# Attention and feed-forward layer: score tiles in runs of three, two and three pairs, and the products with V of two steps together

## The reference, cut to what matters

```python
q, k, v = split(x @ w_qkv.T + b_qkv)          # 16 heads of 16 channels
q, k = rope(elu(q) + 1), rope(elu(k) + 1)
attn = softmax(einsum('bhnd,bhmd->bhnm', q, k) / 4) # 1024 x 1024 for each head
a = einsum('bhnm,bhmd->bhnd', attn, v) + depthwise_conv3(v)
x = layernorm(x + a)
h = relu(s0 * [x, -x] @ W0) * 2               # 512 -> 1024, weights +1 or -1
h = relu(s1 * h @ W1) * 2                     # 1024 -> 1024
x = layernorm(x + s2 * h @ W2)                # 1024 -> 256
```

## Time and profile before

| | us |
|---|---|
| median of 3 runs | 2095.07 (2094.85 to 2098.65) |
| the profiled execution | 2094.53 |
| its span, first to last instruction | 2092.4 |
| PE busy | 2043.8 (98%), clock granted 0.985 on the mean |
| DVE busy | 1685.7 (81%) |
| ACT busy | 1489.0 (71%) |
| POOL busy | 1013.3 (48%) |

### The profile page before, as it was taken

The page is one execution under the profiler, slowest core; times in us unless marked ns, Lnnn a source line. Parts: engine busy times, 40 slices in busy tenths (PEclk is TensorE's granted clock), DMA queues, the critical chain, the costliest instruction groups (busy, mean ns, idle before and its releaser), DMA issues.

```text
span 2092.4 us, 43715 instructions
## 1 busy us (share of the span) xinstructions
PE 2043.8 (98%) x17150; PEld 802.9 (38%) x17150; DVE 1685.7 (81%) x3094; ACT 1489.0 (71%) x2867; POOL 1013.3 (48%) x583
## 2 busy tenths in 40 slices
PE   5999999999999999999999999999999999999998
PEld 3132323343433434334343343434343343434355
DVE  8989988788887988888887888878888788888143
ACT  3399888766877678776787767777687766867642
POOL 2968287614757158462585328661475704300010
PEclk7699999999999999999999999999999999999999
DMA  5001210020010200021000200002001010000000
GB/s 199 20 17 47 72 24 31 22 72 13 15 37 31 80 16 16 30 77 42 9 27 27 89 22 17 29 16 99 12 17 37 29 62 17 17 9 29 1 21 21
DMA packets 40429, 76.87 MB, mean 37 GB/s; under 512 B 15024, under 2 KB 19488, under 8 KB 37280
## 3 DMA queue, kind: packets, MB, share of 16 engines
q1 hardware_dynamic: 34496, 49.97, 8.3%
q0 software_dynamic: 5184, 23.07, 3.0%
q10 hardware_dynamic: 544, 1.05, 0.1%
HBM read 46.27 MB, written 25.17 MB: 34 GB/s over the span
## 4 chain that ended last, share of the span: by engine, by line
PE 86%; DVE 8%; ACT 3%; issue 1%; SPq 0%; DMA 0%; POOL 0%; POOLq 0%; ACTq 0%
PE unit_banks L761 27%; PE unit_banks L625 22%; PE o_bank L670 22%; PE unit_banks L697 5%; PE unit_banks L774 5%; DVE maxima L1032 5%; ACT probs L855 2%; PE unit_banks L685 2%; PE unit_banks L635 2%; DVE hT L1101 1%; PE unit_banks L678 1%; ACT rows L943 0%; DMA lepe_rows<-in_b_v 0%; ACT work L897 0%; DVE rows L1161 0%
## 5 line engine op out<-in xcount | busy, mean ns | idle before, releaser
L1032 DVE TENSOR_REDUCE maxima<-unit_banks 128x1 f32<-128x512 f32 x2048 | 1302.5, 682 | 285.4 <-PE unit_banks L625 281.7
L855 ACT ACTIVATE probs<-unit_banks 128x512 f32<-128x512 f32 x2048 | 1115.5, 605 | 491.1 <-PE unit_banks L635 487.6
L625 PE MATMUL unit_banks<-k_stack,q_stack 48*128 48x512 f16 x2048 | 636.5, 388 | 6.2 <-DVE maxima L1032 2.7
L635 PE MATMUL unit_banks<-q_stack,k_stack 50*128 50x512 f16 x2048 | 634.0, 383 | 5.3 <-ACT probs L855 3.2
L670 PE MATMUL o_bank<-probs,v_pair 128*32 128x256 f32 x8192 | 565.3, 387 | 4.0 <-issue 4.0
L761 PE MATMUL unit_banks<-h0T,w 128*128 128x512 f16 x2048 | 480.2, 380 | 0.1
L1439 POOL TENSOR_TENSOR attn<-o_rows_sb,rden 128x256 f32<-128x256 f32 x63 | 39.2, 622 | 743.1 <-DVE rden L1045 739.5
L670 PEld LDWEIGHTS o_bank<-probs,v_pair 128*32 128x32 f32 x8192 | 207.0, 109 | 306.3 <-issue 206.0
L625 PEld LDWEIGHTS unit_banks<-k_stack,q_stack 48*128 48x128 f16 x2048 | 121.8, 94 | 433.2 <-issue 241.3
L761 PEld LDWEIGHTS unit_banks<-h0T,w 128*128 128x128 f16 x2048 | 188.6, 98 | 249.3 <-issue 55.6
L1104 DVE SCALAR_TENSOR_TENSOR h1T<-unit_banks,h1T 128x512 f16<-128x512 f32 x128 | 87.3, 682 | 77.9 <-ACT h1T L919 77.8
(11 more groups left out here) (151 smaller groups left out, 1677.8 us busy)
## 6 DMA issues: line engine op xcount, KB each, us to landing
rows<-in_x POOLq DMA_DIRECT2D x8, 1024.0 KB, 6.3
q_stack<-q_scratch SPq DMA_DIRECT2D x128, 64.0 KB, 2.0
k_stack<-k_scratch SPq DMA_DIRECT2D x128, 64.0 KB, 2.0
work<-in_xT SPq DMA_DIRECT2D x7, 1024.0 KB, 8.1
q_scratch<-parts POOLq DMA_DIRECT2D x14, 512.0 KB, 3.3
k_scratch<-parts POOLq DMA_DIRECT2D x14, 512.0 KB, 3.2
out<-rows SPq DMA_DIRECT2D x7, 1024.0 KB, 4.9
q_stack<-q_scratch SPq DMA_DIRECT2D x128, 32.0 KB, 1.9
```

Of the source, the lines that this page charges most:

```text
L625: nc.tensor.matmul(units.out(unit), q_stack[row:row + STACK, r, t * P:(t + 1) * P], k_stack[row:row + STACK, r, half * 512:(half + 1) * 51 ...
L635: nc.tensor.matmul(units.out(unit), k_stack[row:end, r, kt * P:(kt + 1) * P], q_stack[row:end, r, half * 512:(half + 1) * 512], start=True ...
L855: nc.scalar.activation(probs[:, 2 * (kt % 2) + h, half * 512:(half + 1) * 512], units.out(unit), ACT.Exp, scale=exp_regs[2 * (n % PAIRS) + ...
L1032: nc.vector.reduce_max(maxima[:, v // T % 2, h * T + t, half:half + 1], units.out(unit), AXIS_X)\
```

## The change

PE now goes through the steps two at a time. With s odd, and a "pair" one S and one T tile: dense work and own units of step s come behind the first pair of step s; those of step s + 1 come behind its third pair; the products with V of steps s - 1 and s come together behind the second pair of step s + 1. From dense piece to dense piece and to the products this gives runs of two and of three pairs: dense work of s, two pairs, dense work of s + 1, three pairs, products of two steps, three pairs, dense work of s + 2. The function `between(s, i)` names the step whose dense work stands ahead of pair i of step s. A step that has no dense work takes one half product in its place (`early_products`), and the rest follow behind the second pair (`products_behind`).

The readers' orders follow: ACT takes what ended in the dense work ahead of the exponential of the pair behind it, and DVE takes it behind the row maximum of that pair. Side work comes once a step. "max rows" is at kt = 6 instead of 5. `probs` has five halves instead of four, `v_pair` a ring of three pairs instead of four (`copy_v` is one pair less ahead), and `o_rows_sb` one buffer instead of two. The number of matmuls, exponentials, maxima and DMAs is the same, and there are still seven banks.

The diff, unchanged lines and hunks that only rename left out:

```diff
@@ -42,6 +42,8 @@
+V_RING = 3
+HALVES = 5
@@ -65,7 +67,7 @@
-O_ROWS_STEP, RECIPROCAL_STEP, MAX_ROWS_STEP = 2, 3, 5
+O_ROWS_STEP, RECIPROCAL_STEP, MAX_ROWS_STEP = 2, 3, 6
@@ -73,7 +75,7 @@
-COPY_V_AT = {3: (0, 1, 2, 3, 4, 7), 1: (7,), 5: (7,)}
+COPY_V_AT = {3: (0, 1, 2, 3, 4, 5), 1: (7,), 5: (7,)}
@@ -184,14 +186,31 @@
-def done_within(s):
-    return [u for u, part in DEALT[s][:-1] if ends_unit((u, part))] if 0 <= s < STEPS else []
-def done_behind(s):
-    return [u for u, part in DEALT[s][-1:] if ends_unit((u, part))] if 0 <= s < STEPS else []
+def done_in(s):
+    return [u for u, part in DEALT[s] if ends_unit((u, part))]
+def between(s, i):
+    return s if s % 2 == 1 and i == 1 else s + 1 if s % 2 == 1 and i == 3 and s + 1 < STEPS else None
+def early_products(s):
+    if DEALT[s] or s == 0:
+        return []
+    if s % 2 == 1:
+        return [2 * s - 2] if (s - 1) % T != 0 else []
+    return [2 * s - 4 + len(early_products(s - 1))]
+def products_behind(s):
+    return range(2 * s - 4 + len(early_products(s - 1)) + len(early_products(s)), 2 * s) if s > 0 else ()
@@ -223,29 +242,31 @@
-    for s in range(STEPS + 1):
-        for h in range(2):
-            for half in range(2):
-                if s + T + LEAD < STEPS:
-                    yield ("S", s + T + LEAD, h, half), True, True, True
-                if s < STEPS:
-                    yield ("T", s, 1 - h, half), True, True, True
-            if h == 0:
-                for u in done_behind(s - 1):
+    for s in range(STEPS):
+        for i in range(4):
+            w = between(s, i)
+            if w is not None:
+                for u in own_units(w):
+                    yield u, True, True, True
+                for u, part in DEALT[w]:
+                    yield u, part == 0, ends_unit((u, part)), False
+                for _ in early_products(w):
+                    yield PV, False, False, False
+            if s + T + LEAD < STEPS:
+                yield ("S", s + T + LEAD, i % 2, i // 2), True, True, True
+            yield ("T", s, 1 - i % 2, i // 2), True, True, True
+            if w is not None:
+                for u in done_in(w):
...
-                for u in own_units(s) if s < STEPS else ():
-                    yield u, True, True, True
-                for u, part in DEALT.get(s, ()):
-                    ends = ends_unit((u, part))
-                    yield u, part == 0, ends, ends and u not in done_behind(s)
-            elif s > 0:
-                yield PV, False, False, False
+            if i == 1 and s % 2 == 0:
+                for _ in products_behind(s):
+                    yield PV, False, False, False
...
-WRITING = {"S": 0.25, "T": 0.25, "PV": 0.9, "O rows": 0.15, "max rows": 0.15, "scale": 0.1, "bound": 0.1}
+WRITING = {"S": 0.25, "T": 0.25, "PV": 0.45, "O rows": 0.15, "max rows": 0.15, "scale": 0.1, "bound": 0.1}
@@ -344,12 +365,12 @@
-        v_pair = sb("v_pair", [P, RING, T, 2, 32], F32)
+        v_pair = sb("v_pair", [P, V_RING, T, 2, 32], F32)
...
-        probs = sb("probs", [P, 4, N], F32)
+        probs = sb("probs", [P, 2 * HALVES, N // 2], F32)
@@ -380,7 +401,7 @@
-        o_rows_sb = sb("o_rows_sb", [P, 2, 512], F32)
+        o_rows_sb = sb("o_rows_sb", [P, 512], F32)
@@ -636,12 +657,11 @@
-            def scores_both(s, h):
-                for half in range(2):
-                    if s + T + LEAD < STEPS:
-                        scores(s + T + LEAD, h, half)
-                    scores_T(s, 1 - h, half)
+            def score_tiles(s, i):
+                if s + T + LEAD < STEPS:
+                    scores(s + T + LEAD, i % 2, i // 2)
+                scores_T(s, 1 - i % 2, i // 2)
@@ -654,9 +674,10 @@
-            def weighted_v(s, half):
+            def weighted_v(x):
+                s, half = divmod(x, 2)
@@ -665,9 +686,9 @@
-                        p = probs[:, 2 * (kt % 2) + h, half * 512:(half + 1) * 512].rearrange("p (b f q) -> p b f q", f=2, q=P)
+                        p = probs[:, 2 * (x % HALVES) + h].rearrange("p (b f q) -> p b f q", f=2, q=P)
...
-                        done = nc.tensor.matmul(o, v_pair[:, n % RING, kt, h, :], p[:, :, parity, :],
+                        done = nc.tensor.matmul(o, v_pair[:, n % V_RING, kt, h, :], p[:, :, parity, :],
@@ -817,26 +838,24 @@
-                scores_both(s, 0)
-                for unit in own_units(s):
-                    if unit[0] == "O rows":
-                        o_rows(unit)
-                    else:
-                        max_rows_T(unit)
-                for unit, part in DEALT[s]:
-                    dense(unit, part)
-                if s > 0 and not DEALT[s]:
-                    weighted_v(s - 1, 0)
-                    if kt == 0:
-                        weighted_v(s - 1, 1)
-                scores_both(s, 1)
-                if s > 0 and DEALT[s]:
-                    weighted_v(s - 1, 0)
-                    weighted_v(s - 1, 1)
-                elif s > 0 and kt > 0:
-                    weighted_v(s - 1, 1)
-            for half in range(2):
-                weighted_v(STEPS - 1, half)
+                for i in range(4):
+                    w = between(s, i)
+                    if w is not None:
+                        for unit in own_units(w):
+                            if unit[0] == "O rows":
+                                o_rows(unit)
+                            else:
+                                max_rows_T(unit)
+                        for unit, part in DEALT[w]:
+                            dense(unit, part)
+                        for x in early_products(w):
+                            weighted_v(x)
+                    score_tiles(s, i)
+                    if i == 1 and s % 2 == 0:
+                        for x in products_behind(s):
+                            weighted_v(x)
+            for x in range(2 * STEPS - 4 + len(early_products(STEPS - 1)), 2 * STEPS):
+                weighted_v(x)
@@ -844,15 +863,16 @@
-            def exp_probs(s, h, half):
-                n, kt = divmod(s, T)
+            def exp_probs(s, i):
+                n, h, half = s // T, 1 - i % 2, i // 2
+                x = 2 * s + half
...
-                    wait(act, pv_done, 2 * (s - 2) + half + 1)
-                nc.scalar.activation(probs[:, 2 * (kt % 2) + h, half * 512:(half + 1) * 512], units.out(unit), ACT.Exp,
+                    wait(act, pv_done, x - HALVES + 1)
+                nc.scalar.activation(probs[:, 2 * (x % HALVES) + h], units.out(unit), ACT.Exp,
@@ -864,16 +884,16 @@
-                wait(act, attn_written, n - 1)
-                nc.scalar.activation(o_rows_sb[:, n % 2], units.out(unit), ACT.Copy).then_inc(units.free_sem(unit), 1)
+                wait(act, attn_written, n)
+                nc.scalar.activation(o_rows_sb[:], units.out(unit), ACT.Copy).then_inc(units.free_sem(unit), 1)
...
-                wait(act, pv_done, 2 * (n - RING + 1) * T)
-                nc.scalar.activation(v_pair[:, n % RING, :, :, 0:D],
+                wait(act, pv_done, 2 * (n - V_RING + 1) * T)
+                nc.scalar.activation(v_pair[:, n % V_RING, :, :, 0:D],
@@ -958,39 +978,24 @@
-            for n in range(RING):
+            for n in range(V_RING):
...
-            for s in range(STEPS):
+            def side_work(s):
...
-                for half in range(2):
-                    exp_probs(s, 1, half)
-                for unit in done_behind(s - 1):
-                    if unit[0] == "proj":
-                        elu_inputs(unit)
-                if kt == O_ROWS_STEP and n > 0:
-                    copy_o_rows(n - 1)
+                if kt == 0 and n > 0:
+                    copy_o(n - 1)
...
-                    ahead = {1: 1, 3: 2, 5: 3}[kt] if j == PAIRS - 1 else 3
+                    ahead = {1: 1, 5: 2}[kt] if j == PAIRS - 1 else 2
...
-                for unit in done_within(s):
-                    if unit[0] in HIDDEN:
-                        high_part(unit)
-                if b >= 1 and i in NORMALISE_AT[0]:
-                    normalise(b - 1, 0, NORMALISE_AT[0][i])
-                if b >= 2 and i in NORMALISE_AT[1]:
-                    normalise(b - 2, 1, NORMALISE_AT[1][i])
-                for half in range(2):
-                    exp_probs(s, 0, half)
-                for unit in done_behind(s):
-                    if unit[0] in HIDDEN:
-                        high_part(unit)
-                if kt == 0 and n > 0:
-                    copy_o(n - 1)
+                for which in range(2):
+                    if b > which and i in NORMALISE_AT[which]:
+                        normalise(b - 1 - which, which, NORMALISE_AT[which][i])
@@ -999,6 +1004,21 @@
+            for s in range(STEPS):
+                for tile in range(4):
+                    w = between(s, tile)
+                    if w is not None:
+                        if w % T == O_ROWS_STEP and w > T:
+                            copy_o_rows(w // T - 1)
+                        for unit in done_in(w):
```

(43 more changed lines are left out.)

4 lines of the change are left out of this document (2 added, 2 removed).

## The result

The kernel after takes 2135.7 us (median of 4 runs, 2135.5 to 2138.9), the kernel before 2095.3 (2094.9 to 2098.7): 1.019 times as long, with an interval of 1.018 to 1.020. The profiled execution of after took 2135.5, its span 2133.4, against 2094.5 and 2092.4 before.

What follows compares the result with a forecast made beforehand. From the second batch on PE's own order sets the time; readers bound the first. 2094.5 - 47 (changes of kind) + 92 (bank waits) + 2 (first batch) = 2141.5, rounded to 2140 us, 2.1% slower, range 2115 to 2165.

Steps and rivals of the forecast that it cites:

- The saving: PE, batches 1 to 7: 225 fewer runs of tiles at 0.08, 224 fewer product groups at 0.13, 47 us less.
- The waits by kind: Runs of three: bank of first T 0.66, first S 0.70, "max rows" 1.2, behind a projection 1.7 us each.
- rows 7: Trace of four pairs in the first batch: exponential starts 0.46 behind its T, whose bank is reused 1.11 behind it.
- Rival A: Waits in the runs of three don't bite, only the saving is left: 2045 us, 2.4% faster; chance 0.16.
- Rival B: Only half of the waits at PE, 46 us, cancel the saving: 2094 us, no change; chance 0.15.
- C: DVE or ACT reaches the run's first pair 0.6 us late at 81 places: 2190 us; chance 0.12.
- The middle batch and the sum: Middle batch 248.8 - 6.7 + 13.5 = 255.6 us; whole kernel 2094.5 - 47 + 92 + 2 = 2141.5 us.
- the ends 60 and 130 of the waits: Lower and upper bounds, in us, on the 92 us of added waits in batches 1 to 7.
- Buffers: New ring sizes cost nothing; the single o_rows_sb leaves ACT's wait for POOL covered by about 2 us.
- "max rows" a step later: Covered by 1.4 us in dense steps; in the first batch PE may wait 1 us or so seven times.
- Runs behind joint products: PE's 1.89 us of products let three S tiles be nearly read, so the next run finds its banks: nothing taken.
- TensorE's clock: Granted in full, 2.4 GHz, in the middle batch and kept through waits under 2 us: nothing changed for it.

Runs made afterwards that it cites:

- e3: The kernel before with only the smaller buffers (v_pair a ring of three pairs, a single o_rows_sb): 2095.3 us, 1.000 of before.
- e4: The changed kernel without one of the four S tiles, and its maximum, in every even step: 2062.1 us, 0.984 of before.
- e5: The kernel before without the same S tiles as e4, as its yardstick: 2081.8 us, 0.993 of before.
- e9: e2 with the joint products cut in two where two or more banks are taken ahead of the run of three: 2089.0 us, 0.996 of before.
- e12: e9 with ACT's exponential ahead of a projection's reading, high parts still first: 2078.0 us, 0.992 of before.
- e10: e9 with the joint products cut in two in every pair of steps from the second batch on: 2117.5 us, 1.010 of before.
- e2: The changed kernel with DVE splitting "max rows" ahead of the maximum of the run's first S: 2121.9 us, 1.013 of before.
- e14: The changed kernel with ACT's exponential ahead of a projection's reading, high parts still first: 2131.3 us, 1.017 of before.
- e11: e9 with ACT's exponential ahead of both a projection's reading and a hidden unit's high part: 2107.2 us, 1.006 of before.
- e13: The changed kernel with ACT's exponential ahead of both projections' readings and high parts: 2162.2 us, 1.031 of before.

## Why the prediction was right

**The saving.** Forecast 6.7 us in a middle batch, measured 7.0. 32 runs of tiles fewer gave 2.8, which is 0.09 each (0.08 forecast), 32 groups of products fewer gave 4.2, 0.13 each as forecast.

**The waits by kind.** Forecast 0.66, 0.70, 1.2 and 1.7; measured 0.67 to 0.68, 0.74 to 0.76, 1.23 to 1.24 and 1.76. So rows 7, one place in the first batch, were enough for a price that recurs some hundred times: the readers started 0.42 to 0.46 behind the matmul in the dense batches too. The list of waits has 46 for the maxima, 23 for "max rows" and 35 for the exponential; by hand I had 44, 20 and 42 (the five behind projections among the last). Rival A needed a mean under 0.45 at these places and is out, and with it the count of mode changes alone. Rival B is out by the same numbers.

**C** wanted DVE near its limit. In a middle batch it is busy for 204.6 of 255.7 us, and in the batch that I went through one wait alone, behind "hT", is some half a microsecond over its kind. C is out.

**The middle batch and the sum.** 255.6 forecast, 255.7 measured. This is closer than the terms deserve. The waits in a middle batch are 16.6 and not 13.5: behind "hT" one of 1.17, one dense piece behind a run at 0.51 instead of 0.35, a handful of 0.1 to 0.4 where I took nothing, and some hundredths in each kind and in the bases. Against that I had not taken off the 3.4 of waits which the kernel before has in its own runs and which the new order takes over. The two slips cancel, so the agreement to 0.1 us is luck; that of the kinds is not. Over the kernel the sum gave 47 more, of which I took 45, and 40.4 came. The last full batch gave 4.4 where the middle ones gave 6.9, and the stretch behind it 0.8 less than before; the first batch gave +1.9 (2 forecast). Two figures of the working don't fit its own terms. With 0.01 more for each change the saving ends at 52 and not at 54. And the ends 60 and 130 of the waits would give 2110 and 2180, where I wrote 2115 to 2165 as the forecast's own range. The result doesn't hang on either.

**What I costed at nothing.** Buffers: nothing (e3). "max rows" a step later: six waits for the loading of its maxima into `q_stack`, all in the first batch and each 0.5 or less of PE's idle time, where I had allowed for 1 us or so seven times. Runs behind joint products: nearly nothing, some 1 us a batch. TensorE's clock: as often low as before, though elsewhere (the last section). That it stays high through waits under 2 us was read from 230 to 260 us alone; the same trace has it at the lower level near 311.

**Changes of kind against readers.** A middle batch got 7.0 us back for 64 changes of kind less, and paid 13.2 more for banks that the readers had not given back. With one S tile less in a run (e4 against e5) the first decides, with all of them the second. I had weighed the Trainium skill, "TensorEngine Tiling (Array Packing)", section "Key Properties" (a change of tiling mode drains TensorE) against its section "PSUM Bottleneck" (tiling speeds up the matmuls and not the emptying of PSUM). The traces agree with both as far as these numbers go; that the tenth of a microsecond at a change is a drain, no run here shows.

**What stays open.** The 17 us by which e9 missed: five waits a batch behind projections explain them only in part (e12 brought back 11). The readers' new order was never run with PE's old order alone; e10 comes nearest. In after itself it accounts for what e2 and e14 brought back, 13.8 and 4.4 us; at the waits of 0.67 and 0.74 the reader started as early as in the earlier trace rows, so its order has no part in them. Another choice of banks than the code's own was not tried.

## What to carry to other kernels

Before making a run of matmuls longer, count banks: what the run writes, plus units held half done, plus what stands unread ahead of it and what wants a bank right behind it. In this kernel saving a change of kind was worth a tenth of a microsecond, and waiting for a tile of the same run cost two thirds. Cut the run where the count is over, and only there: never cut it took 2135.7 us (2121.9 with e2's order on DVE), cut where crowded 2089.0, cut everywhere 2117.5. On the readers' engines, put ahead of a bank-freeing instruction only work that another in-order engine waits for (the high part), and behind it all that nobody waits for (the projection's reading): e12 and e11 differ in nothing else, and by 29 us.

## What the runs showed of the hardware that I had not expected

A wait of PE can cost twice. The second middle batch above is 1.65 us longer than the others. It has the same wait of 1.76 behind a projection as the batch before it, and there the granted clock fell. PE's timeline, and the windows of that run with its products (1295.53) and of its twin a batch earlier (1039.83):

```profile
1295.53 0.60 PE L656 MATMUL unit_banks<-q_stack,k_stack 50*128 50x512 f16 x2
...
1297.71 0.39 PE L656 MATMUL unit_banks<-q_stack,k_stack 50*128 50x512 f16 x1 [1.36 <-ACT probs L875]
1298.03 3.52 PE L691 MATMUL o_bank<-probs,v_pair 128*32 128x256 f32 x32
1301.48 0.44 PE L646 MATMUL unit_banks<-k_stack,q_stack 48*128 48x512 f16 x1
```
```profile
1295.53:1301.48 5.95, 4.59 (x40) 1.76 (x40) 3.27 (x8) 3.10 (x6) 5.71 (x4) 0.72 0.06 12
1039.83:1043.90 4.07, 2.71 (x39) 1.23 (x38) 3.27 (x8) 3.10 (x6) 3.91 (x3) 1.00 0.02 5
```

(The twin's window ends 0.29 ahead of the next tile, which starts at 1044.19; so 4.36 compares with 5.95.) After 1.36 us idle the joint products take 3.52 instead of 1.93, and the granted clock of a stretch in them is the 1.2 GHz level, back at 2.4 GHz from 1302 on:

```profile
1298.80:1301.20 2.40, 2.40 (x28) 1.03 (x20) 0.19 (x1) 0.00 (x0) 2.32 (x2) 0.50 0.07 13
1302.00:1304.40 2.40, 2.40 (x16) 0.81 (x12) 2.40 (x5) 1.56 (x3) 2.32 (x2) 1.00 0.38 96
```

But the same wait of 1.76 a batch earlier was not followed by it (the second window of the pair), nor any of 1.24 and less in the batch that I went through. In the total it makes no difference here: between 120 and 2060 us the trace of after has this one stretch, worth 1.6 us, and that of before has one too, behind some waits near 311 us, worth about as much.

The other traces have between none (e14) and two such stretches, except e13 with six. At 1.6 each they cost it 10 us, and four of them stand right behind its four waits of 2.0 us, its longest. Of the five waits of 1.76 one was followed by such a stretch in after and one in e2, which has the same five. A long wait isn't needed either: e3, in the old order, has one at 1051 us, in a batch that took 250.4 instead of 248.8, and in the 4 us ahead of it PE was busy for 3.41 and none of its gaps was over 0.3 us. So what sets it off, at one wait and not at its twin, no run tells.
